# Causal mask of the attention maxima: added by VectorE in the instruction that takes the maxima, in place of mask products on TensorE

## What is computed

```python
x = x + attn_a(_layernorm(x))
x = x + ffn(_layernorm(x))
x = x + attn_b(_layernorm(x))
x = x + ffn(_layernorm(x))
```

```python
scores = einsum('bhqd,bhkd->bhqk', q, k) * scale
scores = where(k_pos > q_pos, -inf, scores)      # causal
m = max(scores, axis=-1)
p = softmax(scores - m)
out = p @ v
```

## Time and profile before

| what | value |
|---|---|
| median of 3 runs | 1706.22 us (1706.15 to 1710.4) |
| span of the profiled execution, first to last instruction | 1702.2 us |
| own time of the profiled execution | not given apart from its span; the span lies 4.0 us under the median of the runs |
| PE busy | 1652.0 us, 97%, 19619 products |
| PEld busy | 649.9 us, 38% |
| DVE busy | 1499.0 us, 88%, 2880 instructions |
| ACT busy | 1316.0 us, 77% |
| POOL busy | 828.6 us, 49% |
| DMA | 59.39 MB, mean 35 GB/s |

### The profile page before, as it was taken

One profiled execution on the slowest core, in us unless ns is written; L12 is line 12 of the kernel. 1 busy time (PEld: TensorE's weight loads), 2 busy tenths in 40 slices (PEclk: granted clock), 3 DMA queues, 4 the chain that ended last, 5 costly groups with the idle time before them and its releaser, 6 DMA issues.

```text
span 1702.2 us, 48542 instructions
## 1 busy us (share of the span) xinstructions
PE 1652.0 (97%) x19619; PEld 649.9 (38%) x19619; DVE 1499.0 (88%) x2880; ACT 1316.0 (77%) x2638; POOL 828.6 (49%) x1175
## 2 busy tenths in 40 slices
PE   8889999999999999999999999999999999999998
PEld 6655544444344333334333333332332222222324
DVE  6858987998999999999999999999999999999702
ACT  2435677666877787887878888888889989899894
POOL 3257888786766754746636415414142213001341
PEclk9999999999999999999999999999999999999999
DMA  4143113214111211130111210100030000000000
GB/s 109 45 88 57 48 46 72 44 31 70 44 25 49 45 37 25 39 56 25 34 26 23 44 24 20 31 12 14 14 56 24 12 14 19 2 2 14 14 20 20
DMA packets 120390, 59.39 MB, mean 35 GB/s; under 512 B 71909, under 2 KB 120165, under 8 KB 120165
## 3 DMA queue, kind: packets, MB, share of 16 engines
q1 hardware_dynamic: 117924, 55.23, 15.1%
q10 hardware_dynamic: 2240, 1.05, 0.5%
HBM read 24.26 MB, written 16.25 MB: 24 GB/s over the span
## 4 chain that ended last, share of the span: by engine, by line
PE 63%; DVE 21%; ACT 6%; POOL 4%; issue 3%; SPq 2%; DMA 2%; ACTq 0%; POOLq 0%; DVEq 0%
PE psum L2270 20%; DVE span_max L1938 17%; PE psum L2217 12%; PE psum L2249 11%; PE psum L2007 6%; PE psum L1999 5%; PE psum L2018 4%; ACT probs L1623 3%; PE psum L2028 1%; DMA rows<-rows 1%; PE psum L2224 1%; DVE span_max L1932 1%; PE psum L2279 1%; ACT probs L1634 1%; DVE small L1780 1%
## 5 line engine op out<-in xcount | busy, mean ns | idle before, releaser
L1938 DVE TENSOR_REDUCE span_max<-psum 128x1 f32<-128x512 f32 (+1 forms) x2048 | 1241.6, 670 | 60.7 <-PE psum L2217 44.2
L1623 ACT ACTIVATE probs<-psum 128x512 f32<-128x512 f32 (+3 forms) x1806 | 886.5, 570 | 161.2 <-PE psum L2249 157.5
L2217 PE MATMUL psum<-k_stack,q_stack 48*128 48x512 f16 (+3 forms) x2304 | 557.6, 364 | 7.5 <-DVE span_max L1938 4.4
L2249 PE MATMUL psum<-q_stack,k_stack 50*128 50x512 f16 (+3 forms) x2304 | 542.4, 364 | 4.3 <-DMA q_stack<-shift_rows 1.0
L2270 PE MATMUL psum<-probs,v_aug 128*17 128x512 f32 (+3 forms) x3936 | 484.7, 565 | 1.2 <-ACT oT L1643 1.0
L2217 PEld LDWEIGHTS psum<-k_stack,q_stack 48*128 48x128 f16 x2304 | 162.8, 93 | 330.6 <-DVE span_max L1938 240.1
L2249 PEld LDWEIGHTS psum<-q_stack,k_stack 50*128 50x128 f16 x2304 | 150.8, 93 | 322.6 <-ACT probs L1623 179.3
L1461 POOL TENSOR_SCALAR_AFFINE_SELECT probs<-probs 128x512 f32<-128x512 f32 x116 | 74.0, 641 | 243.7 <-ACT probs L1623 234.1
L1623 ACT ACTIVATE w_gates<-psum 128x512 f32<-128x512 f32 (+1 forms) x280 | 139.7, 559 | 18.0 <-PE psum L2249 17.6
L2270 PEld LDWEIGHTS psum<-probs,v_aug 128*17 128x17 f32 x3936 | 67.4, 95 | 124.8 <-issue 110.5
L2224 PE MATMUL psum<-mask_keys,mask_rows 64*128 64x64 bf16 x1024 | 87.8, 189 | 0.0
(11 more groups left out here) (193 smaller groups left out, 1728.8 us busy)
## 6 DMA issues: line engine op xcount, KB each, us to landing
q_stack<-q_parts SPq DMA_DIRECT2D x192, 32.0 KB, 2.0
k_stack<-k_parts SPq DMA_DIRECT2D x42, 128.0 KB, 4.6
rows<-in_x SPq DMA_DIRECT2D x16, 256.0 KB, 2.7
q_parts<-rows SPq DMA_DIRECT2D x32, 128.0 KB, 1.9
k_parts<-rows SPq DMA_DIRECT2D x32, 128.0 KB, 2.0
out<-rows SPq DMA_DIRECT2D x16, 256.0 KB, 2.2
x_rows<-rows SPq DMA_DIRECT2D x14, 256.0 KB, 2.4
rows<-x_rows SPq DMA_DIRECT2D x14, 256.0 KB, 2.8
```

Source lines behind the costliest of these rows:

```text
L1623: act.activation(probs_of(tile)[:, i, q0:], bank(b)[:, q0:], ACT.Exp, scale=SCALE / QK_SCALE).then_inc(exp_done, 1)
L1938: nc.vector.tensor_reduce(span_max[:, s % SPAN_RING, row:row + 1, k0 // SPAN:k0 // SPAN + 1], bank(b)[:, 0:k1 - k0], AX.X, ALU.max).then_i ...
L2217: ins = nc.tensor.matmul(bank(b)[:, at:at + k1 - k0], q_stack[row:row + SCORE_ROWS, s % Q_RING, v, qt * P:(qt + 1) * P], k_stack[row:row + ...
L2249: nc.tensor.matmul(bank(b)[:, q0:], k_stack[row:row + STACK, g * PAIRS + u, j * P:(j + 1) * P], q_stack[row:row + STACK, s % Q_RING, u, q0 ...
```

## The change

DVE no longer takes the maximum of a last span with `tensor_reduce`. It uses `tensor_tensor_reduce`, which adds a second tensor (`mask_ends`, bfloat16 in SBUF: 0, and -1e30 above the diagonal in its last 128 columns), writes the sums back over the scores in the bank, and gives the maximum through its accumulator output. One such call takes one pair, so that a shared bank needs two. PE issues no mask products; `m_full` is raised by the product itself. The tables `mask_rows` and `mask_keys` and the nine POOL instructions that fill them go; a memset and a selection for `mask_ends` come. `span_max` has 2 slots in place of 3. The planner is not touched, so ORDER is the same.

```diff
-SPAN_RING = 3
+SPAN_RING = 2
...
-        mask_rows = sb("mask_rows", [P, 2, P], BF16)
-        mask_keys = sb("mask_keys", [P, HALF], BF16)
+        mask_ends = sb("mask_ends", [P, SPAN], BF16)
...
-                settle(nc.gpsimd.memset(mask_rows[:], 0.0))
-                settle(nc.gpsimd.memset(mask_keys[:], 0.0))
...
+                settle(nc.gpsimd.memset(mask_ends[:], 0.0))
+                const(nc.gpsimd.affine_select(out=mask_ends[:, SPAN - P:], in_=mask_ends[:, SPAN - P:],
+                                              compare_op=ALU.is_ge, fill=MASKED, base=0, pattern=[[-1, P]],
+                                              channel_multiplier=1))
...
                     dve.wait_ge(m_full[half], m + 1)
-                    if u == BOTH:
-                        row = qt * HG + half
-                        nc.vector.tensor_reduce(
-                            span_max[:, s % SPAN_RING, row:row + HG - 1:2, k0 // SPAN:k0 // SPAN + 1],
-                            bank(b)[:, 0:PAIRS * (k1 - k0)].rearrange("p (u k) -> p u k", u=PAIRS),
-                            AX.X, ALU.max).then_inc(span_reduced, 1)
+                    if k1 == (STEPS[s][1] * TT + qt + 1) * P:
+                        if s == 0 and qt == 0:
+                            dve.wait_ge(consts_ready, 3)
+                        n = k1 - k0
+                        for i, v in enumerate(range(PAIRS) if u == BOTH else (u,)):
+                            row = qt * HG + v * 2 + half
+                            scores_at = bank(b)[:, i * n:(i + 1) * n]
+                            ins = nc.vector.tensor_tensor_reduce(
+                                out=scores_at, in0=scores_at, in1=mask_ends[:, SPAN - n:], scale=1.0, scalar=2 * MASKED,
+                                op0=ALU.add, op1=ALU.max, accum_out=span_max[:, s % SPAN_RING, row, k0 // SPAN:k0 // SPAN + 1])
+                        ins.then_inc(span_reduced, 1)
...
-                            pe.wait_ge(consts_ready, 4)
+                            pe.wait_ge(consts_ready, 2)
...
-                                               start=True, stop=not ends)
-                        if ends:
-                            for n in range(2):
-                                k = at + k1 - P - k0 + n * HALF
-                                ins = nc.tensor.matmul(bank(b)[:, k:k + HALF], mask_rows[row:row + HALF, n],
-                                                       mask_keys[row:row + HALF], start=False, stop=(n == 1))
+                                               start=True, stop=True)
```

More of the change, by code:

```diff
@@ L1202, in constants @@
                                               pattern=[[-1, P]], channel_multiplier=1))
-                settle(nc.gpsimd.memset(mask_rows[:], 0.0))
-                settle(nc.gpsimd.memset(mask_keys[:], 0.0))
-                for half in range(2):
-                    own = slice(half * HALF, (half + 1) * HALF)
-                    for n in range(2):
-                        settle(nc.gpsimd.affine_select(out=mask_rows[own, n], in_=mask_rows[own, n],
-                                                       compare_op=ALU.not_equal, fill=1.0, base=HALF * n - 1,
-                                                       pattern=[[-1, P]], channel_multiplier=1))
-                    ins = nc.gpsimd.affine_select(out=mask_keys[own], in_=mask_keys[own], compare_op=ALU.is_gt,
-                                                  fill=MASKED, base=0, pattern=[[-1, HALF]], channel_multiplier=1)
-                    if half == 0:
-                        settle(ins)
-                    else:
-                        const(ins)
-                for half in range(2):
-                    ins = nc.gpsimd.memset(mask_rows[half * HALF:half * HALF + 1, 1, 0:HALF], 1.0)
-                    if half == 0:
-                        settle(ins)
-                    else:
-                        const(ins)
+                settle(nc.gpsimd.memset(mask_ends[:], 0.0))
+                const(nc.gpsimd.affine_select(out=mask_ends[:, SPAN - P:], in_=mask_ends[:, SPAN - P:],
+                                              compare_op=ALU.is_ge, fill=MASKED, base=0, pattern=[[-1, P]],
+                                              channel_multiplier=1))
             def raised(ln, eps=EPS, unit=1.0):
@@ L2211, in _ @@
                         if c == 0:
-                            pe.wait_ge(consts_ready, 4)
+                            pe.wait_ge(consts_ready, 2)
                     row = HALF * half
-                    ends = k1 == (c * TT + qt + 1) * P
                     for i, v in enumerate(range(PAIRS) if u == BOTH else (u,)):
```

## The result

The changed kernel takes **1719.34 us** (median, 1717.31 to 1720.33) where the kernel before takes 1706.18: a ratio of 1.0084, 95% interval [1.0062, 1.0106]. A second series gave 1718.29 and a ratio of 1.0076 [1.0059, 1.0092]; all nine runs have a median of 1718.33. It is slower, by 13 to 14 us; forecast were 18, within 1697 to 1790. The profiled execution took 1720.33 us, its span is 1718.5.

The account below looks back on a forecast made before the run. PE and DVE were both taken as near their limit after 400 us, DVE setting the pace in 800:1200. DVE's extra +26.6, PE's relief -8 and POOL's start -0.5 made +18 on 1706.2: 1724 us, range 1697 to 1790.

Parts of the forecast that it names:

- Split banks: On DVE, shared banks need one sum for each pair, in place of one reduction for both: 8 us in 32 steps.
- A sum priced as a reduction: On DVE, each new sum was to occupy as much as a reduction of its width, 0.60 us at 512 columns.
- The rival of a slow instruction: On DVE, sums at two cycles a column would cost 171 us more, the time about 1886 us; chance 0.07.
- Reads at 0.09 us: On DVE, each of 512 accumulator reads occupies 0.09 us, like an aggregate: 46 us in 32 steps.
- The shares that reach the end: Parts of DVE's 54 us extra lengthening the time: a quarter, half, nine tenths, half over four stretches; together 26.6 us.
- in 100:400 there is 2.6 times as much room, a quarter shows: Stretch 100 to 400 us: DVE's idle 52.7 us against 20.0 us extra, so only 5.0 us reaches the end.
- PE's relief, -8: On PE, 1024 mask products leave; half of their 17 us on the chain was counted, -8 us, bounds 0 and -17.
- POOL's start, -0.5: At the start, fewer mask constants let POOL's first operation of the order begin before 5.93 us: -0.5 us.
- The break-even read of 52 ns: The read's price on DVE at which extra work of 35 us, half on the path, balances PE's whole 17 us.
- the rival of PE's relief: Reads cost about 0.02 us, 6 us shows, PE gains the whole 17: faster, 1695 us; chance 0.17.
- The rival without overlap: On DVE, sum and read do not overlap: up to 131 us extra, time about 1762, or 1790 us; chance 0.14.
- What would show it: Signs in the profile after: DVE busy near 1550 us, idle under 3 in 800:1200, longer weight-load waits, PE busy less.

Follow-up runs that it names:

- relief alone: The kernel before without its 1024 mask products on PE, nothing else changed; 1697.63 us, ratio 0.9961.
- the copy: The changed kernel without its accumulator reads, with a one-column copy between SBUF tiles behind each of the 512 sums; 1722.07 us, ratio 1.0087.
- relief without constants: The kernel before without its mask products and without the POOL instructions that build the two mask tables; 1699.7 us, ratio 0.9967.

## Why the prediction was right, and where not

The direction was right for the reason given: the change takes work from the engine that waits more and gives it to the one that waits less. The size, 18 forecast and 13 measured, is right by luck: two errors cancel.

- **Split banks, 8 us of DVE: right.** Measured 8.1 (1496.1 to 1504.2).
- **A sum priced as a reduction: right.** 0.60 us at 512 columns, and 2.8 us in 512 sums, 5 ns each. The rival of a slow instruction is out; the rule of the Trainium skill ("Vector Engine (DVE) Microarchitecture Reference", section 7) on two SBUF sources that are not bfloat16 did not bite, as the prediction had it: one source here is in PSUM and one bfloat16, and the trace agrees. That the write back into the bank costs nothing, which the prediction gave without a row, is in the same figure.
- **Reads at 0.09 us: wrong, the mis-sized term.** 29 ns, so 14.6 us in place of 46. I went by the aggregates, since a read has to wait until the maximum is complete. The read's row is as long as theirs (145 ns, 158 there), but the next instruction's row starts together with it. The value lay near the low end, the memsets' 0.02; where sums follow each other it is 0.05. DVE's extra is 25.5 us over relief alone, not 54. The Trainium skill ("Vector Engine (DVE) Microarchitecture Reference", section 5.2) gave 49 us by its 75 ns for each instruction; the trace does not agree for the read, nor for the copy with its 26.0/512 = 51 ns.
- **The shares that reach the end: ½, 0.9 and ½ right, the first wrong.** From relief alone to the changed kernel (the marks of both profiles above) steps 0 to 11 lose 13.1 and 11.3 us, 12 to 19 lose 3.5 and 3.6, 20 to 25 lose 5.0 twice, 26 to 31 lose 3.1 and 2.8. The extra is 25.5/32 = 0.80 a step, 9.6, 6.4, 4.8 and 4.8 us. So the shares are 1.2 to 1.4, 0.55, 1.04 and 0.6. The first is not that sure: from relief without constants the first steps lose 5.8 and 7.6 us, a share of 0.6 to 0.8, and by the times the sums in the first twelve steps cost 2.9 to 4.9 us over plain reductions. The four together make 0.9 to 1.0, more than the 0.8 of the medians, since the profiled execution of relief alone was its fastest and the first of the changed kernel its slowest. What holds is that the sums of steps 0 and 1 cost 5 us, as much as was forecast for the whole stretch from twice the extra. **The step that failed is "in 100:400 there is 2.6 times as much room, a quarter shows".** DVE does idle there for 52.7 us, but not where the sums stand: in steps 0 and 1 PE waits for exactly these maxima, and then its clock falls too. The prediction's sum has no term for the clock.
- **PE's relief, -8: right by itself, -6.6** (from the interval 4.6 to 8.7). It is not a term that can be added: with DVE's cost in place and PE given its products back, the time is only 1.8 us longer than without them.
- **POOL's start, -0.5: right.** Its first operation of the order comes at 5.43 us in place of 5.93; nothing of it can be measured in the time.
- **The sum.** With the read's true price and the shares as forecast, 25.5 x 26.6/54 = 12.6, less 8.5, would have been +4, a wash. With the true share and my price, 54 x 0.81 = 44, less 8.5, +35. The break-even read of 52 ns under the rival of PE's relief rested on a half of the extra on the path and a relief of 17; at four fifths, and with a relief of 6.6, the read's 29 ns lose all the same. (The rival without overlap was also added up wrongly: two thirds of 131 us, less 8.5, give 1785, not 1790.)
- **What would show it.** Right: the weight loads' wait (301 us, after 257), and the reductions' and sums' share of the chain (18% to 29%), though relief alone moves both the same way (272 us, 21%) and is faster. Wrong: DVE near 1550 (1521.6), PE's busy time down by tens of us (up by 11.5; products at the lower level of the clock are part of it, the rest wasn't looked into), DVE idle under 3 us in 800:1200 (4.6; in a fixed window a bound engine looks the same however slow it is, and the chain, 68% against 53% with relief alone, tells more).

What stays open: how much of the 13 us the clock takes. The changed kernel's mean clock is 0.9907, that of before 0.9946. Over the 74 runs of the kernel before in these series, the time falls by 1.5 us for 0.001 more of mean clock (correlation -0.82): by that, 5 to 6 us of the 13. It is more likely too high than too low, since a run that waits more may have a lower clock for that reason. Nor does the clock alone order the kernels: relief without constants has 0.9918 and is faster than before.

## What to carry over

Before work is moved between two engines that are both near their limit, price the instructions that come with it (an accumulator is read by one of its own) by the distance between starts, not by the row's length, and count relief and cost together: the relief of the engine that waits is worth little once the other is loaded. An engine's idle time in a stretch is cover only if it lies where the added work stands; look at the first steps of a pipeline on their own, where little overlaps and the added instructions lie on the chain. Compare kernels by the start of one recurring instruction, step by step: it shows where a loss of 1% may arise. But take two profiles of each kernel first, since here two of the same work lay up to 5 us apart, and confirm the place with a kernel that leaves the work out there.

## What the runs showed of the hardware

- The maximum of a two-tensor sum with accumulator is fetched by a second instruction. Its row is 145 ns, the room it takes 29 ns on average and 0.05 us between sums that follow each other; a copy of one column has 147 ns and 51 ns.
- Such a sum (one source in PSUM, float32, one in SBUF, bfloat16, written back to PSUM) costs a reduction's time: 0.60 us at 512 columns.
- A subtraction of two SBUF tensors on DVE and a like instruction on POOL lengthen each other when they meet: 0.68 us becomes 1.43 to 1.62 for DVE when POOL has started first, 1.15 becomes 1.55 to 1.68 for POOL when DVE has (fourteen profiles, eight and six).
- The granted clock reacted to the change (mean of the runs 0.9946 before, 0.9907 after). In 130:140 PE was busy for all of 10 us in both kernels, and the clock was 0.94 before and 0.70 after the change, where in the 10 us ahead of it PE had been busy for 8.76 and 7.97 us:

```profile
120.00:130.00 10.00, 8.76 (x98) 5.12 (x89) 9.47 (x19) 2.60 (x7) 5.50 (x5) 0.89 0.34 84
130.00:140.00 10.00, 10.00 (x273) 7.84 (x271) 5.93 (x18) 3.65 (x7) 5.30 (x9) 0.94 0.01 4
```

```profile
120.00:130.00 10.00, 7.97 (x91) 4.37 (x83) 7.62 (x28) 3.52 (x8) 8.20 (x10) 0.96 0.33 85
130.00:140.00 10.00, 10.00 (x143) 5.22 (x146) 6.34 (x24) 1.29 (x3) 3.62 (x7) 0.70 0.05 3
```

It is no rule: the kernel with sums in the first twelve steps had PE busy for 7.98 us in 120:130 and then a clock of 0.93.

- PE's busy time rose by 11.5 us with 1024 products fewer (1652.0 to 1663.5), and that comes from DVE's side: without the sums it falls to 1645.6, and with the sums and zero products in place it is 1669.8.
